# Scaling the router's logits inside their PSUM bank, adding the bias from the bank, and one signal for both events

## The reference, cut to what matters

```python
rms = jnp.sqrt(jnp.mean(xf * xf, axis=-1, keepdims=True) + EPS)
xn = xf / rms * norm_weight
logits = xn @ router_weight.T + router_bias
probs = jax.nn.softmax(logits, axis=-1)
_, idx = jax.lax.top_k(logits.T, top_k)
```

## Time and profile before

| | |
|---|---|
| median of 3 runs | 1117.07 us |
| the profiled execution: its time, its span | 1117.18 us, 1115.4 us |
| PE busy | 992.3 us, 89% |
| DVE busy | 820.4 us, 74% |
| POOL busy | 786.8 us, 71% |
| ACT busy | 672.7 us, 60% |

### The profile page before, as it was taken

One profiled execution on the slowest core, in us unless ns is written; L12 is line 12 of the kernel. 1 busy time (PEld: TensorE's weight loads), 2 busy tenths in 40 slices (PEclk: granted clock), 3 DMA queues, 4 the chain that ended last, 5 costly groups with the idle time before them and its releaser, 6 DMA issues.

```text
span 1115.4 us, 17736 instructions
## 1 busy us (share of the span) xinstructions
PE 992.3 (89%) x6102; PEld 654.7 (59%) x6102; DVE 820.4 (74%) x1908; ACT 672.7 (60%) x1335; POOL 786.8 (71%) x880
## 2 busy tenths in 40 slices
PE   3899999899998999999998999899740699999996
PEld 3665556455654645565565565444320589999995
DVE  7989858877776886787788678665778776666642
ACT  6855865677565665858666765544436336666662
POOL 4137986687887789588879967888714267777773
PEclk9899999999999999999999999999965699999998
DMA  6020020002001201100300000001027176666662
GB/s 188 1 62 1 2 62 20 1 1 65 1 1 44 68 10 43 44 21 2 83 21 1 21 27 1 22 1 52 2 69 225 58 147 212 209 204 201 201 166 24
DMA packets 73753, 71.94 MB, mean 64 GB/s; under 512 B 38944, under 2 KB 67712, under 8 KB 69568
## 3 DMA queue, kind: packets, MB, share of 16 engines
q1 hardware_dynamic: 66608, 62.05, 18.3%
q0 software_dynamic: 6272, 8.69, 4.6%
q10 hardware_dynamic: 784, 0.07, 0.1%
HBM read 56.96 MB, written 13.83 MB: 63 GB/s over the span
## 4 chain that ended last, share of the span: by engine, by line
PE 74%; DVE 10%; POOL 7%; ACT 3%; issue 3%; DMA 3%; SPq 0%; ACTq 0%; DVEq 0%; POOLq 0%
PE bank L913 40%; PE score_pair L913 17%; PE pair_bank L913 12%; POOL prob_sum L1496 6%; DVE c_in L1939 2%; ACT probs L1223 2%; PE bank L946 2%; PE bank L994 1%; DMA gathered<-rows_scratch,token_index 1%; DVE masked_scores L1818 1%; DMA rows_scratch<-all_probs 1%; DMA v_nat<-in_w_lat 1%; PE score_pair L1171 1%; PE bank L982 1%; DVE maxima L1811 1%
## 5 line engine op out<-in xcount | busy, mean ns | idle before, releaser
L1496 POOL TENSOR_TENSOR prob_sum<-prob_sum,probs 128x256 f32<-128x256 f32 x628 | 466.5, 774 | 65.3 <-ACT probs L1223 58.3
L1223 ACT ACTIVATE probs<-score_pair,mask_col 128x512 f32<-128x512 f32 x256 | 161.9, 685 | 103.8 <-PE score_pair L913 94.8
L1818 DVE CUSTOM_DVE_ANT_0 masked_scores<-pair_bank,mask_bias 128x512 bf16<-128x512 f32 x248 | 160.6, 685 | 57.4 <-PE pair_bank L913 57.1
L913 PE MATMUL bank<-probs,v_nat 128*64 128x512 f32 x768 | 195.5, 616 | 0.0
L1223 ACT ACTIVATE probs<-score_pair 128x512 f32<-128x512 f32 x128 | 69.5, 596 | 76.1 <-PE score_pair L913 74.5
L1811 DVE TENSOR_REDUCE maxima<-pair_bank 128x2 f32<-128x1024 f32 x62 | 75.5, 1217 | 45.6 <-PE pair_bank L913 45.4
L913 PE MATMUL score_pair<-q_hi,k_hi 64*128 64x512 f32 x384 | 91.4, 468 | 10.2 <-ACT probs L1223 6.9
L913 PEld LDWEIGHTS bank<-probs,v_nat 128*64 128x64 f32 x768 | 45.4, 137 | 84.1 <-issue 81.1
L913 PE MATMUL pair_bank<-k_hi,q_hi 64*128 64x512 f32 x372 | 86.4, 457 | 6.6 <-DVE maxima L1811 4.6
L913 PEld LDWEIGHTS score_pair<-q_hi,k_hi 64*128 64x128 f32 x384 | 37.7, 185 | 80.8 <-ACT probs L1223 58.3
L1571 POOL DMA_INDIRECT out_x<-y_out,token_index x32 | 54.7, 1709 | 39.3 <-DVE y_out L2137 34.6
(11 more groups left out here) (270 smaller groups left out, 2561.6 us busy)
## 6 DMA issues: line engine op xcount, KB each, us to landing
w_raw<-in_fc SPq DMA_DIRECT2D x16, 1024.0 KB, 4.8
w<-in_fc SPq DMA_DIRECT2D x16, 1024.0 KB, 5.6
c_in<-in_ctx SPq DMA_DIRECT2D x16, 384.0 KB, 4.0
x_in<-in_x SPq DMA_DIRECT2D x8, 512.0 KB, 6.3
out_x<-x_in SPq DMA_DIRECT2D x8, 512.0 KB, 3.0
rows_scratch<-xr_nat SPq DMA_DIRECT2D x8, 512.0 KB, 3.0
c_in<-in_ctx SPq DMA_DIRECT2D x16, 128.0 KB, 4.5
b_rows<-in_fc_bias SPq DMA_DIRECT2D x16, 128.0 KB, 5.7
```

Source lines behind the costliest of these rows:

```text
L913: return pe.matmul(out, lhsT, rhs, start=start, stop=stop, skip_group_check=True)
L1223: return act.activation(out, a, f, bias=bias, scale=scale)
L1496: last = tt(total[:, half], first[:, half], p[:, half], ALU.add)
L1818: last = dve.tensor_tensor_reduce(masked[:, hh, :], place[:, hh, :], mask_bias[:, 512 * g:512 * (g + 1)], 1.0, MASKED, ALU.add, ALU.max, m ...
```

## The change

The multiplication writes its product back into the bank, and a `settle` waits for it. The addition then reads the bank and the bias, writes `logits_of(b)`, and raises the bank's "emptied" semaphore. The signal `logits_scaled` goes away; who waited for it waits for that "emptied" value.

```diff
-    logits_scaled, centred_logits = signal("logits_scaled"), signal("logits_centred")
+    centred_logits = signal("logits_centred")
...
         def route_back(b):
             use = ("route_back", b)
             on.wait_ge(*misc.vacant(*use))
-            on.wait_ge(*logits_scaled.at(b))
+            on.wait_ge(*misc.emptied("route_logits", b))
...
         def route_weigh(b):
             on.wait_ge(*x_normed.at(b))
             if b == B - 1:
-                on.wait_ge(*logits_scaled.at(b))
+                on.wait_ge(*misc.emptied("route_logits", b))
...
-            tt(logits_of(b), misc.bank(*use)[:, 0:MT * E].rearrange("p (j e) -> p j e", j=MT),
-               root_y[:, ROWS:N_ROOTS].unsqueeze(2).broadcast_to(shape), ALU.mult).then_inc(misc.empty(*use), 1)
-            on.wait_ge(*misc.emptied(*use))
-            tt(logits_of(b), logits_of(b), router_b[:].unsqueeze(1).broadcast_to(shape),
-               ALU.add).then_inc(logits_scaled.sem, 1)
+            made = misc.bank(*use)[:, 0:MT * E].rearrange("p (j e) -> p j e", j=MT)
+            settle(tt(made, made, root_y[:, ROWS:N_ROOTS].unsqueeze(2).broadcast_to(shape), ALU.mult))
+            tt(logits_of(b), made, router_b[:].unsqueeze(1).broadcast_to(shape), ALU.add).then_inc(misc.empty(*use), 1)
...
         def soft_max(b):
-            on.wait_ge(*logits_scaled.at(b))
+            on.wait_ge(*misc.emptied("route_logits", b))
...
         def store_logits(b):
-            on.wait_ge(*logits_scaled.at(b))
+            on.wait_ge(*misc.emptied("route_logits", b))
```

More of the change, by code:

```diff
@@ L746, in _build @@
                         "row_max": row_max_made,
-                        "sum": last_added, "scale_logits": logits_scaled,
-                        "soft_max": centred_logits, "soft": gates_made}
+                        "sum": last_added, "soft_max": centred_logits, "soft": gates_made}
     for kind, *at in vector_plan:
```

## The result

The changed kernel takes 1113.83 us (median of 12 runs), the kernel before 1117.28 us (12 runs beside them). The ratio is 0.9974, with a 95% interval of 0.9962 to 0.9986: 2.9 us faster, 1.6 to 4.2. The two medians alone are 3.45 us apart; where this text names a gain over the kernel before, it goes by the ratio. The predicted gain of 4.29 us is a ratio of 0.9962, at the edge of that interval. The predicted time was 1112.8 us, with a range of 1111.0 to 1115.3; the measured one lies in the range, 1.0 us above the forecast. The profiled execution took 1114.77 us, with a span of 1112.6 us.

What follows compares the result with a forecast made beforehand. PE was taken as the bound, with one wait for DVE's held-up addition in batch 1. Wait 2.57 plus slow clock 1.72 us, together 4.29, off 1117.18 gave 1112.9, predicted as 1112.8; range 1111.0 to 1115.3.

Steps and rivals of the forecast that it cites:

- One wait of PE for DVE bounds, at batch 1: In the attention, of PE's three waits for plain maxima, 4.6 us, one of 2.6 us stands behind batch 1's addition.
- The addition of 5.11 us is a wait for POOL, because of its second SBUF input: Batch 1, line 1890: POOL holds up the addition; with one SBUF input it takes 0.22 us.
- Rival B: Batch 1's addition is still held up, as the number of SBUF inputs doesn't count: no change, 1117.0 us; chance 0.08.
- PE's wait of 2.57 us goes whole: Batch 1: the plain maximum ends near 344.8, before PE comes at 345.83, so 2.57 us are gained.
- The hold-up moves to the subtraction, and is hidden: Batch 1, line 1912: up to 1.9 us instead of 0.66, hidden from PE by 0.5 us.
- Rivals C and D: Batch 1's subtraction is held longer: to POOL's run's end, 1120.2 us, chance 0.06; or one pause later, 1115.1, chance 0.07.
- The slow clock behind the wait, 1.72 us: From 349.80 to 353.30 the clock was 0.51; without the wait it stays at 2.4 GHz, gaining 1.72 us.
- rival A: The wait goes but the slow clock doesn't, coming at a denominator instead: −2.57 us, 1114.5 us; chance 0.14.
- all of it moves along: After batch 1's denominator POOL waits for ACT, which waits for PE, so everything behind comes earlier with PE.
- The additions of the other batches: Batches 0, 2, 3, 4 and 5: shorter additions, counted as nothing, at best 0.3 us.
- the longer hold of the bank: The bank is held to the end of the addition, about 0.26 us; nothing waits, cost 0.
- the write back: The multiplication writes the bank it reads; on the path only in the last batch, 0 to +0.3 us, taken as 0.

Runs made afterwards that it cites:

- the run with another tile: The kernel before, with the product of the first six batches in the SBUF tile `soft`, so the addition isn't in place: 1117.08 us, 0.9998.
- the two memset runs: The changed kernel with four or ten memsets on DVE behind batch 1's addition: 1114.46 us (0.9980) with four, 1121.85 us (1.0047) with ten.
- the signals alone: The changed kernel, but with the product going to SBUF, so the addition has two SBUF inputs: 1119.10 us, 1.0010.

## Why the prediction was right, step by step

*One wait of PE for DVE bounds, at batch 1.* Shown, mainly by the profiles: with batch 1 alone changed 3.9 of the 4.6 us come in the attention, with all the others changed none.

*The addition of 5.11 us is a wait for POOL, because of its second SBUF input.* Shown from both sides. With the input taken away it lasts 0.22 us; with the input kept and a pause of 0.08 us made in POOL it lasts 2.42 us. That it had to wait for a pause was not so: in two of the five profiles with the wait it was let in one sum earlier, at a change without a pause, after 4.47 us. Rival B (still held up) is excluded by the rows of line 1888, and that being in place was the cause by the run with another tile.

*PE's wait of 2.57 us goes whole.* Shown. DVE has 2.3 us to spare there, by the two memset runs. The prediction's times give the same: DVE free at 342.3 for scores ready near 343.5, and done at 344.8 for a PE that comes at 345.83.

*The hold-up moves to the subtraction, and is hidden.* It started at 345.14 on the old scale (345.2 predicted) and took 1.32 us (at most 1.9). PE did not wait. The prediction let it in at POOL's next pause; it got in earlier, at 346.46 on that scale, at a change without a pause. Rivals C and D did not happen.

*The slow clock behind the wait, 1.72 us.* Here the prediction's step is half right. In the profiled pair it went as said, 0.51 before and 1.00 after. But its place is not fixed. The kernels that keep the wait can be compared with those that don't by the time from batch 0's denominator sum to batch 5's, which leaves the uneven start out. First the kernel before, again, and the changed one, again:

```profile
218.05:702.77 484.72, 467.48 (x2688) 272.79 (x2689) 372.56 (x843) 321.05 (x634) 387.66 (x480) 0.99 0.10 27
```

```profile
216.19:696.49 480.30, 465.68 (x2688) 272.32 (x2689) 365.04 (x843) 320.73 (x634) 387.44 (x480) 1.00 0.10 27
```

The five kernels with the wait (before twice, the signals alone, all but batch 1, the other tile) take 484.7, 484.7, 485.1, 485.3 and 485.4 us; the five without it (after twice, batch 1 alone, POOL's pause, four memsets) take 480.2, 480.3, 480.9, 481.6 and 480.9. The means are 485.1 and 480.8, a difference of 4.3 us. That is the predicted sum, although in four of the five profiles with the wait the clock did not fall right behind it but at a denominator, and in the last two of them the wait itself was only 1.9 to 2.0 us. So rival A is right that the slow stretch can fall elsewhere, but in the profiles that did not eat the gain: kernels with the wait had on average one slow stretch more, three or four between 200 and 780 us against two or, in one case, three.

*The size.* The timed gain is 2.9 us, then 3.5 us, and the predicted 4.29 lies at the edge of the first interval and within the second. In the attention the profiles have the whole sum, 4.3 us, as said. What is missing lies where the prediction put nothing:

- Behind batch 5's denominator sum it has "all of it moves along". From there to the end of the span the five kernels with the wait take 413.9 to 414.8 us, the five without it 414.6 to 415.9. The means are 414.2 and 415.1, so 0.9 us are lost again. Why, no run shows.
- The measured time also holds a part outside the span. It is 1.81 us on average in the kernel before and never over 1.88, and 2.17 in the changed one and never under 2.12, so 0.36 us more. Why is open as well.

Together they are 1.3 us, about what the timed gain, 3.2 us on average, lacks of 4.29.

The executions that were only timed agree. Each has its span and its mean granted clock on record. For 90 executions of the kernel before these are 1115.5 us and 0.9534 on average, for 24 of the changed kernel 1111.9 us and 0.9549. The spans differ by 3.6 us. As an estimate, the time lost to the clock is the span times what the clock lacks of 1: 52.0 us before and 50.1 after, some 1.8 us less. So the clock's 1.72 us are there on average too, and it is not the clock's term that came out too large.

*The additions of the other batches, the longer hold of the bank, the signals, the write back.* Counted at nothing, and worth nothing that can be told by the runs with the signals alone and with all but batch 1; the longer hold costs 0.35 us of PE's time only where the addition is still held up. The write back cost 8 ns of the 0 to 0.3 us allowed, and PE's wait in the last batch is 1.77 us, against 1.76.

```profile
818.04 0.66 PE L1097 MATMUL bank<-ident,squares 128*128 128x128 f32 x4 [1.77 <-DVE squares L1888]
```

## What to carry to other kernels

Look for instructions of one form whose longest row is many times their shortest: they are waits that the profile books as work. Here one row of 5.1 us out of eight was the whole case, and the median told nothing of it. A small DVE instruction between PE and its next bank should have at most one input in SBUF while POOL runs back to back on SBUF tiles; where it can't, a short pause of POOL at the right instruction does as well, and a wait of PE that no engine can shorten can be filled by moving the waiting instruction behind work that is ready.

## What the runs showed of the hardware that was not expected

A DVE addition with two SBUF inputs that meets POOL instructions without a gap between them can be held for several of them: 5.1 us, through `xr_nat` and four sums. It gets in about 0.08 us after the end of one of them. A pause of 0.08 us in POOL was always enough (17 of 17); without one it was let in at 67 changes and held on at 57. The shortest addition of this form before took 257 ns.

The price of a wait of PE depends on more than its length. In two profiles of the same kernel the slow stretch fell behind different waits, 2.6 us at batch 1 in the one and 1.9 us at batch 2's denominator in the other. Both profiles have both waits.
